# A Perceiver layer on one core: the last two tiles' banks, halves and feature sums, and two layer norms whose scale moves behind the products

## The chip, the core and the metric

The kernel runs on one core of a Trainium2 chip. The metric is the device time of one execution in microseconds, from which a median over runs is taken. Lower is better.

The engines are named as the profile names them: PE is the matrix engine (its weight loads, PEld, overlap with its products), DVE the vector engine, ACT the scalar engine, POOL the general engine, and SP the one whose queue issues most of the DMAs.

## The reference

One latent block x of 128 rows by 512 columns goes through three layers, each of the form x = x + f(layernorm(x)):

```python
# 1: linear cross attention over 12544 context rows, 16 heads of 32, 64 features
q, k, v = heads(layernorm(x) @ Wq.T + bq), heads(ctx @ Wk.T + bk), heads(ctx @ Wv.T + bv)
q_prime, k_prime = relu(q @ Wqf.T), relu(k @ Wkf.T) * mask
kv    = einsum('nf,ne->fe', k_prime, v)      # sum over the 12544 rows, per head
k_sum = sum(k_prime)                         # the same sum of the features alone
x = x + (q_prime @ kv) / (q_prime @ k_sum + 1e-8) @ Wo.T + bo
# 2: gated running average, then a gated feed forward
q, k, v = split(rms(layernorm(x)) @ w_qkv.T); q, k = rms(q), rms(k); w = exp(k)
y = sigmoid(q) * cumsum(w * v) / (cumsum(w) + 1e-6)
u, g = split(y @ w_swiglu.T);  x = x + (u * silu(g)) @ w_out.T
# 3: two experts, the better one weighted by its softmax share, activation max(h, h/2)^2
x = x + share * (max(h, h / 2) ** 2) @ w_proj[e].T     where h = layernorm(x) @ w_fc[e].T
```

## The kernel before

The program is written engine by engine: each engine has its own instruction list, and semaphores order them. Nothing is scheduled automatically, so the order on an engine is the order of the source.

**The long part (0 to about 735 us).** The context comes in 98 tiles of 128 rows, numbered 0 to 97 (NT = 98), four to a period. Per tile PE makes the values (4 steps of 3 products, in `v_bank`, a bank of PSUM), the keys of a tile ahead (in `k_bank`), the features (4 jobs of 2 products in `f_ps`, `feature_job`), and the key-value sums of the tile before (`key_values`, 8 products into `kv_ps`). ACT and DVE empty the banks: for each of the 4 jobs ACT copies a share (`fb`) and DVE adds it (`features_sum`), DVE masks the tile's features (`masked_features`), and ACT and DVE split them into a high and a low part (`features_high`, `features_low`) that `key_values` takes. POOL adds the masked features of each tile onto `ksum_acc`. A feature job i waits until DVE has added job i - 2, since two banks alternate.

**The last two tiles, 96 and 97.** There are no keys left to make, so `values_last` puts one feature job behind each value step. The values of tile 96 go into `k_bank`, those of 97 into `v_bank`. POOL still adds tile 96 onto `ksum_acc`. Then `feature_sums` sums `ksum_acc` and tile 97's features over rows with products against a tile of ones, and the last `key_values` follows.

**The tail (about 754 us to the end).** One chain over 128 rows: denominator and numerator of the attention, the product with Wo (L776), a layer norm, the q, k, v products, two running sums, the feed forward with `hidden_down` (4 calls, all summed in one bank, `down_ps`), a layer norm, the router, and the experts with 8 more calls of `hidden_down`. `turn` transposes a 128x512 block on PE in two halves, `turned` copies them back on DVE. `keep_warm(n)` issues n products whose result nobody reads, while PE would be waiting for the vector chain (L773, L777, L828). These products are full fp32, each of which runs as two instructions. Both layer norms of the tail have DVE take the moments (L1039 to L1042, and L869 to L871), then POOL raise the variance to the power -1/2 (L321), then DVE write (x - mean) * scale in two halves, which `turn` waits for. In the q, k, v part, POOL adds a constant `rms_eps` to the mean squares of k and q (L385).

SP issues the large weight transfers of the tail after the last `key_values`. The names of the semaphores say what they count (`kf_ready`: tiles of masked features; `kv_done`: tiles summed).

## Time and profile before

| | |
|---|---|
| median of 3 runs | 897.54 us (897.27 to 897.81) |
| the profiled execution, its own time | 898.03 us |
| its span, first to last instruction | 896.2 us |
| PE busy in the span | 881.7 us (98%) |
| DVE, ACT, POOL busy | 617.6, 509.3, 369.0 us |
| PE's share of the chain that ended last | 89% |
| granted PE clock, mean | 1.000 |

The execution's own time is its span and about 1.8 us around it. Busy shares are means over a span with two very different stages, the 98 tiles and the tail; the chain of work that ended last says which engine the end waited for at each moment. A granted clock of 1.00 is 2.4 GHz.

### The profile page before, as it was taken

The numbers are of one execution on the slowest core, as the hardware profiler recorded it, in microseconds if no ns is written. First come the engines' busy times: TensorE is split into PE (matmuls) and PEld (weight loads), VectorE is DVE, ScalarE is ACT, GpSimd is POOL, SyncE is SP. The second block draws the span as 40 slices with busy tenths as digits, with TensorE's granted clock in tenths as the row PEclk, the third lists the DMA queues.
The fourth block names the chain that finished last, engine by engine and source line by source line (L and its number), as shares of the span: only waits on it lengthen the run. The fifth ranks groups of instructions, "written<-read, shape, count | busy, mean of one in ns | idle before, by whom it ended". The sixth has DMA issues, their size and how long they took to land.

```text
span 896.2 us, 14101 instructions
## 1 busy us (share of the span) xinstructions
PE 881.7 (98%) x4486; PEld 708.6 (79%) x4486; DVE 617.6 (69%) x992; ACT 509.3 (57%) x916; POOL 369.0 (41%) x212
## 2 busy tenths in 40 slices
PE   8999999999999999999999999999999998999998
PEld 6888888888888888888888888888888887344443
DVE  5777777777777777777777777777777786522422
ACT  5566666666666666666666666666666663100000
POOL 4445555555554444444444444554555341000000
PEclk9999999999999999999999999999999999999999
DMA  6222121212010101010101010101010002936400
GB/s 237 89 77 76 67 81 60 86 55 90 27 47 23 47 23 47 23 47 23 47 23 47 23 47 23 47 23 47 23 48 24 1 28 118 443 146 278 188 1 12
DMA packets 12550, 64.12 MB, mean 72 GB/s; under 512 B 1904, under 2 KB 2672, under 8 KB 11376
## 3 DMA queue, kind: packets, MB, share of 16 engines
q1 hardware_dynamic: 11808, 63.58, 19.1%
q10 hardware_dynamic: 720, 0.25, 0.1%
q8 instruction: 13, 0.21, 0.1%
q14 instruction: 9, 0.07, 0.0%
HBM read 63.56 MB, written 0.26 MB: 71 GB/s over the span
## 4 chain that ended last, share of the span: by engine, by line
PE 89%; issue 6%; DVE 2%; DMA 2%; ACT 1%; SPq 0%; POOL 0%; POOLq 0%; DVEq 0%; ACTq 0%
PE kv_ps L634 10%; PE f_ps L624 10%; PE v_bank L547 10%; PE v_bank L548 10%; PE k_bank L547 10%; PE v_bank L549 10%; PE k_bank L548 10%; PE k_bank L549 9%; PE kv_ps L805 3%; PE v_bank L702 2%; PE k_bank L702 2%; DMA x_sb<-in_x 1%; PE k_bank L688 1%; DVE kf L912 0%; DVE keys L882 0%
## 5 line engine op out<-in xcount | busy, mean ns | idle before, releaser
L335 POOL TENSOR_TENSOR ksum_acc<-ksum_acc,kf 128x1024 f32<-128x1024 f32 x97 | 233.9, 2412 | 193.0 <-DVE kf L906 188.5
L430 ACT ACTIVATE fb<-f_ps 128x256 f32<-128x256 f32 x392 | 149.7, 382 | 177.3 <-PE f_ps L624 171.0
L899 DVE TENSOR_TENSOR kf<-f_ps,fb 128x256 f32<-128x256 f32 x392 | 165.3, 422 | 111.2 <-ACT fb L430 106.0
L328 POOL TENSOR_TENSOR ctx_lo<-ctx_raw,ctx_hi 128x512 fp32r<-128x512 f32 x94 | 123.1, 1310 | 177.7 <-ACT ctx_hi L405 177.7
L624 PEld LDWEIGHTS f_ps<-bd,keys 128*128 128x128 f32 x784 | 146.2, 188 | 35.1 <-DVE kf L899 2.4
L624 PE MATMUL f_ps<-bd,keys 128*128 128x256 f32 x784 | 156.0, 281 | 2.2 <-DVE kf L899 2.2
L547 PE MATMUL v_bank<-wv_hi,ctx_lo 128*128 128x512 f32 x388 | 153.2, 395 | 0.0
L547 PE MATMUL k_bank<-ctx_hi,wk_lo 128*128 128x512 f32 (+1 forms) x392 | 152.8, 390 | 0.0
L548 PE MATMUL v_bank<-wv_lo,ctx_hi 128*128 128x512 f32 x388 | 152.6, 393 | 0.0
L548 PE MATMUL k_bank<-ctx_lo,wk_hi 128*128 128x512 f32 (+1 forms) x392 | 152.2, 388 | 0.0
L549 PE MATMUL v_bank<-wv_hi,ctx_hi 128*128 128x512 f32 x388 | 150.9, 389 | 0.0
L912 DVE TENSOR_TENSOR kf<-kf 128x1024 fp32r<-128x1024 f32 x98 | 122.0, 1245 | 42.0 <-ACT kf L436 42.0
L549 PE MATMUL k_bank<-ctx_hi,wk_hi 128*128 128x512 f32 (+1 forms) x392 | 149.9, 382 | 0.0
L413 ACT ACTIVATE keys<-k_bank,bias_cols 64x512 fp32r<-64x512 f32 (+1 forms) x194 | 131.1, 676 | 30.8 <-PE k_bank L549 28.4
L882 DVE SCALAR_TENSOR_TENSOR keys<-k_bank,bias_cols,keys 64x512 fp32r<-64x512 f32 (+1 forms) x194 | 143.3, 738 | 6.3
L634 PEld LDWEIGHTS kv_ps<-kf,v 128*128 128x128 f32 x784 | 106.3, 189 | 8.4 <-DVE v L890 0.3
L634 PE MATMUL kv_ps<-kf,v 128*128 128x256 f32 x784 | 109.1, 282 | 0.2 <-DVE v L890 0.2
L436 ACT ACTIVATE kf<-kf 128x1024 fp32r<-128x1024 f32 x98 | 103.9, 1061 | 3.6 <-DVE kf L906 1.3
L549 PEld LDWEIGHTS k_bank<-ctx_hi,wk_hi 128*128 128x128 f32 x392 | 73.7, 188 | 15.8
L549 PEld LDWEIGHTS v_bank<-wv_hi,ctx_hi 128*128 128x128 f32 x388 | 72.9, 188 | 16.4
L906 DVE TENSOR_SCALAR kf<-kf,mask 128x1024 f32<-128x1024 f32 x98 | 73.9, 754 | 10.9
L547 PEld LDWEIGHTS k_bank<-ctx_hi,wk_lo 128*128 128x128 f32 x392 | 73.6, 188 | 9.6 <-issue 0.7
(185 smaller groups left out, 792.0 us busy)
## 6 DMA issues: line engine op xcount, KB each, us to landing
ctx_raw<-in_ctx SPq DMA_DIRECT2D x48, 512.0 KB, 3.3
early<-in_early SPq DMA_DIRECT2D x14, 512.0 KB, 4.3
swi_b<-in_swib SPq DMA_DIRECT2D x1, 4096.0 KB, 14.1
w_out<-in_wout SPq DMA_DIRECT2D x1, 4096.0 KB, 23.4
fc<-in_fc SPq DMA_DIRECT2D x1, 4096.0 KB, 34.1
early<-in_proj SPq DMA_DIRECT2D x1, 4096.0 KB, 12.3
swi_b<-in_fc SPq DMA_DIRECT2D x1, 4096.0 KB, 12.3
w_out<-in_proj SPq DMA_DIRECT2D x1, 4096.0 KB, 13.4
```

The costliest lines, as they stand in the source:

```text
L328: pool.tensor_tensor(ctx_lo[:, s, :, cols], ctx_raw[:, :, t % 2 * P:(t % 2 + 1) * P], ctx_hi[:, s, :, cols].bitcast(f32), ALU.subtract).th ...
L335: pool.tensor_tensor(ksum_acc[:, :].rearrange("p (j f) -> p j f", f=P), ksum_acc[:, :].rearrange("p (j f) -> p j f", f=P), kf[:, t % 2, :, ...
L413: act.activation(keys_2[rows, s, 2 * m + h, 0:n], src[rows, 0:n], ACT.Identity, bias=bias_cols[rows, KC + m:KC + m + 1]).then_inc(k_hi_rea ...
L430: act.activation(fb[:, i % 2, :, :], f_ps[i % 2][:, :].rearrange("p (j x f) -> p j x f", j=2, x=2) [:, :, 1, :], ACT.Copy).then_inc(fb_rea ...
L547: pe.matmul(out_ps, st_lo, mv_hi, start=start, stop=False, **kw)
L548: pe.matmul(out_ps, st_hi, mv_lo, start=False, stop=False, **kw)
L549: return pe.matmul(out_ps, st_hi, mv_hi, start=False, stop=stop, **kw)
L624: last = pe.matmul(f_ps[i % 2][:, (j % 2) * 2 * P:(j % 2 + 1) * 2 * P], keys_2[:, s, j, t * P:(t + 1) * P], bd[:, :, :].rearrange("p x f - ...
L634: last = pe.matmul(kv_ps[:, j, :, :].rearrange("p x f -> p (x f)"), v_2[:, t % 2, j, :, :].rearrange("p x e -> p (x e)"), kf_2[:, t % 2, j ...
L882: dve.scalar_tensor_tensor(out=keys_2[other, s, 2 * m + h, 0:n], in0=src[rows, 0:n], scalar=bias_cols[rows, KC + m:KC + m + 1], in1=keys_2 ...
L899: dve.tensor_tensor(kf[:, t % 2, 2 * i:2 * i + 2, :], f_ps[i % 2][:, :].rearrange("p (j x f) -> p j x f", j=2, x=2)[:, :, 0, :], fb[:, i % ...
L912: dve.tensor_tensor(kf_2[:, t % 2, :, 1, :], kf[:, t % 2, :, :], kf_2[:, t % 2, :, 0, :].bitcast(f32), ALU.subtract)\
```

## The change

1. **Banks.** The values of tile 96 go into `v_bank`, those of tile 97 into `k_bank` (before, the other way round), and the feature sums with the denominator's input into `v_bank`.
2. **Order on ACT and DVE in these two tiles.** The values are emptied between feature jobs 2 and 3, where before they came after all four.
3. **Feature sums on PE.** POOL no longer adds tile 96. PE sums `ksum_acc` in two pieces inside tile 97's values, then tile 96's features, then tile 97's: 8 products more.
4. **Tile 97's features in two halves**: mask, high and low part, sums and key-value sums are each done for pairs 0 to 3 and then 4 to 7.
5. **Layer norm scales behind the products.** In both layer norms of the tail DVE writes only x - mean, and `turn` no longer waits for POOL. The scale is multiplied in later: into v's product with the exponentials, into `rms_eps` (now a column that DVE computes), into the router's logits, and its square into the expert shares.
6. **Column halves.** The product with Wo and every `hidden_down` is made as two products of 256 columns in two banks. The adds and moments (`centered`) take each half as it is done. The last call of each sum finishes half 0 before it starts half 1. `keep_warm` goes from 4 to 1 and from 3 to 1. The output's halves are added and stored as they are done.

```diff
@@ banks @@
-        k_ps, v_ps, down_ps = [k_bank[:, :], v_bank[:, :]], [kv_bank[1], kv_bank[2]], kv_bank[0]
+        k_ps, v_ps = [k_bank[:, :], v_bank[:, :]], [kv_bank[1], kv_bank[2]]
+        o_ps = [v_bank[:, 0:D // 2], kv_bank[1][:, 0:D // 2]]
+        half_ps = [kv_bank[0][:, 0:D // 2], kv_bank[3][:, 0:D // 2]]
@@ POOL @@
-            period(LAST, 0, last=True, splits=0)
@@ ACT @@
+            def tile_last(n, t):
+                features_share(n, 0, False)
+                features_high(n - 1, t - 1)
+                for i in (1, 2):
+                    features_share(n, i, False)
+                values_high(n, t, False, k_bank if t else v_bank)
+                features_share(n, 3, False)
@@ PE @@
             def values_last(n, s, t, jobs):
-                if t == 0:
+                pe.wait_ge(v_lo_ready, n - t)
+                if t == 1:
                     pe.wait_ge(k_lo_ready, 2 * KC * (LAST + 1))
-                else:
-                    pe.wait_ge(v_lo_ready, n - 1)
                 for k in range(KC):
-                    value_step(n, s, t, k, k_bank if t == 0 else v_bank)
+                    value_step(n, s, t, k, k_bank if t else v_bank)
                     feature_job(*jobs[k])
+                    if t == 1 and k in (1, 2):
+                        if k == 1:
+                            pe.wait_ge(v_lo_ready, NT - 1)
+                            pe.wait_ge(ksum_added, NT - LAST_TILES)
+                        feature_sums(0, k - 1)
...
-                feature_sums()
-                key_values(NT - 1, LAST_TILES - 1, last_tile=True)
+                for b in range(2):
+                    feature_sums(1, b)
+                for b in range(2):
+                    pe.wait_ge(kf_ready, NT + b)
+                    last = feature_sums(2, b)
+                last.then_inc(ksumT_done, 1)
+                pe.wait_ge(v_lo_ready, NT)
+                for b in range(2):
+                    pe.wait_ge(kf_lo_ready, NT + b)
+                    for j in range(b * NPAIR // 2, (b + 1) * NPAIR // 2):
+                        last = key_value(j, 1, False, True)
+                    last.then_inc(kv_done, 1)
...
-            rows(k_ps[1], act_T, w_o, 0, turned=1).then_inc(o_done, 1)
-            keep_warm(4)
+            for b in range(2):
+                rows(o_ps[b], act_T, w_o, b * D // 2, turned=1, n=D // 2).then_inc(o_done, 1)
+            keep_warm(1)
...
-                for k in range(KC):
-                    last = pe.matmul(down_ps, hid_T2[n % 2][:, k, :], w[:, at + k, :],
+                for b, k in ([(b, k) for b in range(2) for k in range(KC)] if last_one else
+                             [(b, k) for k in range(KC) for b in range(2)]):
+                    last = pe.matmul(half_ps[b], hid_T2[n % 2][:, k, :], w[:, at + k, b * D // 2:(b + 1) * D // 2],
...
-            keep_warm(3)
+            keep_warm(1)
@@ DVE @@
+            def tile_last(n, t):
+                features_sum(n, t, 0, False)
+                features_low(n - 1, t - 1)
+                for i in (1, 2):
+                    features_sum(n, t, i, False)
+                values_low(n, t, k_bank if t else v_bank)
+                features_sum(n, t, 3, False)
+                if t < LAST_TILES - 1:
+                    masked_features(n, t)
...
+            def centered(done, n, ps):
+                for b, cols in enumerate(halves):
+                    dve.wait_ge(done, n + b)
+                    link(dve.tensor_tensor(x1[:, cols], x1[:, cols], ps[b], ALU.add))
+                    link(dve.bn_stats(moments[:, b, :], x1[:, cols]))
+                link(dve.bn_aggr(stat[:, 6:8], moments[:, :, :].rearrange("p b s -> p (b s)")))
+                for cols in halves:
+                    dve.tensor_scalar(att[:, cols], x1[:, cols], stat[:, 6:7], None, ALU.subtract).then_inc(act_ready, 1)
+            centered(o_done, 1, o_ps)
...
+            dve.tensor_scalar(rms_eps[:, :], stat[:, 9:10], RMS_EPS, None, ALU.mult).then_inc(var_ready, 1)
+            turned(2)
             dve.wait_ge(rstd_ready, 2)
...
-            dve.tensor_tensor(wval, v_ps[0], wexp, ALU.mult).then_inc(wval_ready, 1)
+            dve.scalar_tensor_tensor(out=wval, in0=v_ps[0], scalar=stat[:, 9:10], in1=wexp, op0=ALU.mult, op1=ALU.mult)\
...
-            link(dve.tensor_copy(logit[:, 0:2], v_ps[0][:, 0:2]))
+            link(dve.tensor_scalar(logit[:, 0:2], v_ps[0][:, 0:2], stat[:, 8:9], None, ALU.mult))
```

How the instructions stand now. PE at the start of tile 96 (the first two rows are `key_values` of tile 94, the rest values and the first feature job of tile 96), before:

```order
L634 MATMUL kv_ps<-kf,v 128x256 [waits kf_lo_ready,v_lo_ready]
L634 MATMUL kv_ps<-kf,v 128x256 x7
L547 MATMUL k_bank<-wv_hi,ctx_lo 128x512 [waits k_lo_ready]
L548 MATMUL k_bank<-wv_lo,ctx_hi 128x512
L549 MATMUL k_bank<-wv_hi,ctx_hi 128x512
L624 MATMUL f_ps<-bd,keys 128x256 [waits fsum_ready,k_lo_ready]
L624 MATMUL f_ps<-bd,keys 128x256
```

and of the changed kernel:

```order
L648 MATMUL kv_ps<-kf,v 128x256 [waits kf_lo_ready,v_lo_ready]
L648 MATMUL kv_ps<-kf,v 128x256 x7
L553 MATMUL v_bank<-wv_hi,ctx_lo 128x512 [waits v_lo_ready]
L554 MATMUL v_bank<-wv_lo,ctx_hi 128x512
L555 MATMUL v_bank<-wv_hi,ctx_hi 128x512
L635 MATMUL f_ps<-bd,keys 128x256 [waits fsum_ready,k_lo_ready]
L635 MATMUL f_ps<-bd,keys 128x256
```

The bank is another, and the wait is for the values' low part of tile 95 (`v_lo_ready`) where it was for the last keys' low part (`k_lo_ready`).

PE at the end of tile 97: `key_values` of tile 96, feature sums, `key_values` of tile 97, denominator, before:

```order
L634 MATMUL kv_ps<-kf,v 128x256 [waits kf_lo_ready,v_lo_ready]
L634 MATMUL kv_ps<-kf,v 128x256 x7
L649 MATMUL k_bank<-ones,ksum_acc 128x64 [waits ksum_added,v_lo_ready]
L649 MATMUL k_bank<-ones,ksum_acc 128x64 x7
L649 MATMUL k_bank<-ones,kf 128x64 [waits kf_ready]
L649 MATMUL k_bank<-ones,kf 128x64 x7
L634 MATMUL kv_ps<-kf,v 128x256 [waits kf_lo_ready,v_lo_ready]
L634 MATMUL kv_ps<-kf,v 128x256 x7
L744 MATMUL v_bank<-ksum_k,qf_T 128x64 [waits ksum_ready]
L744 MATMUL v_bank<-ksum_k,qf_T 128x64 x7
```

and of the changed kernel, from the same `key_values` on:

```order
L648 MATMUL kv_ps<-kf,v 128x256 [waits kf_lo_ready,v_lo_ready]
L648 MATMUL kv_ps<-kf,v 128x256 x7
L656 MATMUL v_bank<-ones,kf 128x64 x8
L656 MATMUL v_bank<-ones,kf 128x64 [waits kf_ready]
L656 MATMUL v_bank<-ones,kf 128x64 x3
L656 MATMUL v_bank<-ones,kf 128x64 [waits kf_ready]
L656 MATMUL v_bank<-ones,kf 128x64 x3
L648 MATMUL kv_ps<-kf,v 128x256 [waits kf_lo_ready,v_lo_ready]
L648 MATMUL kv_ps<-kf,v 128x256 x3
L648 MATMUL kv_ps<-kf,v 128x256 [waits kf_lo_ready]
L648 MATMUL kv_ps<-kf,v 128x256 x3
L761 MATMUL v_bank<-ksum_k,qf_T 128x64 [waits ksum_ready]
```

Tile 96's features are summed here now (the row without a wait), tile 97's sums and key-value sums are in halves, and the sums of `ksum_acc` have moved up into the values.

DVE around the first layer norm of the tail, from the add of x and bo to the copies of the transposed block, before:

```order
L1032 TENSOR_TENSOR x<-x_sb,bo 128x512
L1034 TENSOR_TENSOR x<-x,v_bank 128x512 [waits o_done,vector_chain]
L1039 BN_STATS stat<-x 128x6 [waits vector_chain]
L1040 BN_AGGR stat<-stat 128x2 [waits vector_chain]
L1041 TENSOR_SCALAR stat<-stat 128x1 [waits vector_chain]
L1042 TENSOR_SCALAR stat<-stat 128x1
L1046 TENSOR_SCALAR att<-x,stat 128x256 [waits rstd_ready]
L1046 TENSOR_SCALAR att<-x,stat 128x256
L1028 COPY act_T<-kv_ps 128x256 [waits actT_done]
L1028 COPY act_T<-f_ps 128x256 [waits actT_done]
```

and of the changed kernel:

```order
L1071 TENSOR_TENSOR x<-x_sb,bo 128x512
L1077 TENSOR_TENSOR x<-x,v_bank 128x256 [waits o_done,vector_chain]
L1078 BN_STATS moments<-x 128x6 [waits vector_chain]
L1077 TENSOR_TENSOR x<-x,kv_ps 128x256 [waits o_done,vector_chain]
L1078 BN_STATS moments<-x 128x6 [waits vector_chain]
L1079 BN_AGGR stat<-moments 128x2 [waits vector_chain]
L1081 TENSOR_SCALAR att<-x,stat 128x256 [waits vector_chain]
L1081 TENSOR_SCALAR att<-x,stat 128x256
L1084 TENSOR_SCALAR stat<-stat 128x1
L1085 TENSOR_SCALAR stat<-stat 128x1
L1086 TENSOR_SCALAR rms_eps<-stat 128x1 [waits vector_chain]
L1067 COPY act_T<-kv_ps 128x256 [waits actT_done]
```

The wait for `rstd_ready` (POOL) ahead of the two writes of `att` is gone, the adds and moments are in halves, and three small operations stand between the second write of `att` and the first copy.

## Rows read from the trace of the kernel before

**Rows 1.** Busy time by window: stretch, its length, PE, PEld, DVE, ACT, POOL, PEclk, DMA, GB/s

```profile
730.00:760.00 30.00, 25.82 (x182) 23.10 (x181) 20.00 (x35) 13.02 (x26) 9.16 (x6) 1.00 0.25 89
...
786.00:829.00 43.00, 42.97 (x112) 19.91 (x113) 8.32 (x13) 3.67 (x5) 0.00 (x0) 1.00 0.52 208
...
835.00:896.00 61.00, 58.12 (x160) 27.00 (x158) 18.32 (x33) 5.08 (x9) 0.00 (x0) 1.00 0.10 39
```

**Rows 2.** Chain of work that ended last, a main-loop tile: start us, us, what

```profile
728.84 0.95 PE kv_ps L634 x8
729.79 0.23 PE v_bank L547
...
730.48 0.24 PE f_ps L624 x2
```

**Rows 3.** Timeline, 734 to 755 us: start, length, engine, operation, count, idle time before it

```profile
734.81 1.12 PE L634 MATMUL kv_ps<-kf,v 128*128 128x256 f32 x8
...
736.31 1.00 DVE L882 SCALAR_TENSOR_TENSOR keys<-k_bank,bias_cols,keys 64x256 fp32r<-64x256 f32 x2
...
737.37 0.50 PE L547 MATMUL k_bank<-wv_hi,ctx_lo 128*128 128x512 f32 x1 [1.44 <-DVE keys L882]
...
738.17 0.40 PE L624 MATMUL f_ps<-bd,keys 128*128 128x256 f32 x2
...
738.61 0.38 ACT L430 ACTIVATE fb<-f_ps 128x256 f32<-128x256 f32 x1 [2.64 <-PE f_ps L624]
...
739.01 1.06 ACT L436 ACTIVATE kf<-kf 128x1024 fp32r<-128x1024 f32 x1
...
739.12 0.42 DVE L899 TENSOR_TENSOR kf<-f_ps,fb 128x256 f32<-128x256 f32 x1 [1.81 <-ACT fb L430]
...
740.11 1.22 DVE L912 TENSOR_TENSOR kf<-kf 128x1024 fp32r<-128x1024 f32 x1 [0.56 <-ACT kf L436]
...
751.00 1.95 PE L649 MATMUL k_bank<-ones,kf 128*128 128x64 f32 x16
...
753.15 1.22 PE L634 MATMUL kv_ps<-kf,v 128*128 128x256 f32 x8 [0.20 <-DVE v L890]
```

**Rows 4.** Waits between 730 and 896 us: who waited for whom, us in total, times, longest

```profile
PE f_ps L624 <- DVE kf L899: 2.0, 2, 1.3
```

**Rows 5.** Timeline of PE and DVE around the first layer norm of the tail

```profile
766.54 3.60 PE L688 MATMUL k_bank<-x_sb,ident 128*128 128x512 f32 x8
...
766.81 0.69 DVE L1034 TENSOR_TENSOR x<-x,v_bank 128x512 f32<-128x512 f32 x1 [3.00 <-PE v_bank L702]
...
767.53 0.69 DVE L1039 BATCH_NORM_STATS2 stat<-x 128x6 f32<-128x512 f32 x1
...
768.26 0.18 DVE L1040 BATCH_NORM_AGGREGATE stat<-stat 128x2 f32<-128x6 f32 x1
...
769.52 0.73 DVE L1046 TENSOR_SCALAR att<-x,stat 128x256 f32<-128x256 f32 x2 [0.83 <-POOL stat L321]
...
769.99 0.44 PE L769 MATMUL kv_ps<-ident,att 128*128 128x128 f32 x2
...
771.03 0.67 PE L702 MATMUL v_bank<-early,act_T 128*128 128x512 f32 x1 [0.28 <-DVE act_T L1028]
```

**Rows 6.** Timeline around the second layer norm of the tail

```profile
829.09 2.74 PE L688 MATMUL k_bank<-x_sb,ident 128*128 128x512 f32 x6
...
829.29 0.69 DVE L1079 TENSOR_TENSOR x<-x,kv_ps 128x512 f32<-128x512 f32 x1 [6.18 <-PE kv_ps L805]
...
832.23 0.44 PE L769 MATMUL kv_ps<-ident,att 128*128 128x128 f32 x2 [0.40 <-DVE att L874]
```

**Rows 7.** Chain of work that ended last, its end: start us, us, what

```profile
886.25 6.88 PE kv_ps L805 x16
```

**Rows 8.** Timeline of DVE at the end of the span

```profile
893.16 0.75 DVE L1107 TENSOR_TENSOR hid<-x,kv_ps 128x256 f32<-128x256 f32 x2 [6.18 <-PE kv_ps L805]
```

**Rows 9.** Groups of PE's instructions by shape: busy us, mean ns, idle time before

```profile
L688 PE MATMUL k_bank<-ksum_acc 128*128 128x512 f32 x12 | 7.5, 787 | 1.9 <-POOL ksum_acc L317 1.9
```

More of the change, by code:

```diff
@@ L337, in add_features, with period @@
                     .then_inc(ksum_added, 1)
[L339 removed]
+            def period(c, s, splits=TILES):
                 n = TILES * c
[L342 removed]
+                for t in range(TILES):
                     if t < splits:
                         split_ctx_low(n + 2 * TILES + t, s, t)
[L345 to L346 removed]
+                    add_features(n + t, t)
             for b in range(2):
@@ L493, in _ @@
             period(LAST - 1, 1, splits=0, keys=HALF)
-            period(LAST, 0, last=True, splits=0)
+            for t in range(LAST_TILES):
+                tile_last(NT - LAST_TILES + t, t)
+            for b in range(2):
+                features_high_last(b)
             act.wait_ge(ksumT_done, 1)
@@ L701, in rows @@
                         pe.wait_ge(actT_ready, 2 * turned - 1 + k // 2)
-                    last = pe.matmul(ps, act_t[:, k, :], w[:, k, at:at + D], start=start and k == 0,
+                    last = pe.matmul(ps, act_t[:, k, :], w[:, k, at:at + n], start=start and k == 0,
                                      stop=stop and k == KC - 1)
@@ L992, in _ @@
             period(LAST - 1, 1, keys=HALF)
-            period(LAST, 0, last=True)
-            dve.wait_ge(kv_done, NT)
+            for t in range(LAST_TILES):
+                tile_last(NT - LAST_TILES + t, t)
+            dve.wait_ge(fsum_ready, JOBS * NT)
+            for b in range(2):
+                masked_features_last(b)
+            for b in range(2):
+                features_low_last(b)
+            dve.wait_ge(kv_done, NT + 1)
             for b in (2, 3):
```

133 lines of the change are left out of this document (58 added, 75 removed).

## The prediction

> **What bounds the kernel now.** I read the page first: PE is busy for 98% of the span. Then I cut the end of the span into windows. From 786 to 829 us PE is busy 42.97 of 43 us, from 835 to 896 us 58.12 of 61, but from 730 to 760 us only 25.82 of 30 [rows 1]. So in the two long product stretches only PE's own pace counts, and what a faster vector chain can win lies where PE waits: around tiles 96 and 97 and around the layer norms. The 96 tiles ahead of 735 us are not touched, and I take them as they are. The chain of work gives PE's pace there: a value step takes 0.69 us (729.79 to 730.48), a feature job 0.24, a `key_values` 0.95 [rows 2]. A timeline row of PE reads longer, since the end of its last product is modelled (1.12 for the same 0.95), so I count from start to start.
>
> The timeline then shows the waits. `key_values` of tile 94 starts at 734.81 and so hands over at 735.76, but tile 96's values start at 737.37, after DVE's last keys (736.31 and 1.00 long) [rows 3]. Two feature jobs wait another 2.0 us for DVE [rows 4], and the last `key_values` starts at 753.15, after 0.20 of wait [rows 3]. In the tail, the products of `keep_warm` only fill the time of the vector chain, which has the same length with or without them [rows 5, 6].
>
> **Part A, tiles 96 and 97.** Before: from 735.76 to 754.10 (753.15 + 0.95) are 18.34 us. The work in it is 8 value steps (5.52), 8 feature jobs (1.92), 3 `key_values` (2.85) and 16 sum products. Eight sum products take about 1.87 (the row says 1.95 with its modelled end [rows 3]), so 3.74, and the work is 14.03. The remaining 4.3 us are waits and slow first products after them.
>
> After, step by step. Values 96 need only `v_bank` free, which is long so: they start at 735.76. The first feature job starts at 736.45. ACT takes its share 0.44 after a job starts (738.17 to 738.61), so 736.89 to 737.27; DVE leaves the keys at 737.31 and adds until 737.8; ACT's high part of tile 95 (1.06) runs until 738.35, DVE's low part (1.22) until 739.6, the second add (0.42, or 0.37 in a queue) until 740.0 [rows 3]. Feature job 3 waits for that add. PE has done its third other job and four value steps at 739.26, so one wait of 0.8 us stays, 1.03 with the slow first product. Behind it I followed every wait in the same way: the next adds are ready 1.1 us or more ahead of the jobs that need them, tile 97's masked first half 0.6 ahead of its sums, and its low parts 1.1 ahead of the last `key_values`. So from 740.04 on PE never waits. The price is one more block of sums, 1.87, all on PE. Sum: 14.03 + 1.87 + 1.03 = 16.93 instead of 18.34, and the last `key_values` starts at 751.74 instead of 753.15: **1.41 us won**. DVE's low part of tile 96 also loses its overlap with POOL's add, but PE does not wait for it. What follows (denominator, transposes, numerator, SP's four weight transfers) moves as one block. ksum's copy on ACT ends at about 752.6, where PE is free at 752.7, so it hides, by 0.1 only. Bounds: 0.6 if one more feature wait of 0.8 us comes in, 1.8 if the remaining wait falls to half.
>
> **Part B, the first layer norm.** Before, from DVE's add at 766.81 to the transposes at 769.99 are 3.18 us: add 0.69, moments 0.69, aggregate 0.18, two small ones, POOL's power, then 0.47 from `att`'s start to the transpose [rows 5]. After, half 0's add and moments run while PE makes half 1. Behind half 1 stand an add of 128x256 (0.42, as the row of that shape [rows 3]), moments of 256 columns, the aggregate 0.18 and three gaps of 0.03. No row has moments of half size: 0.35 (half of 0.69) to 0.69, and I take 0.42, as for the add. That is 1.11, and 1.58 with the 0.47. Gain 1.60. `keep_warm(1)` ends after 0.86 (829.09 and 829.29 show that it starts 0.2 ahead of the add [rows 6]) and is no longer what PE waits in. Against it: three small operations (0.37 together with their wait) stand ahead of the first copy and end 0.2 later than the transpose allows. Part B wins **1.40**. The column halves also make two instructions of 256 columns out of each of 512; that price comes below.
>
> **Part C, the second layer norm.** From the add at 829.29 to the transpose at 832.23 are 2.94 us [rows 6], afterwards again 1.58: gain **1.36**. Here only one small operation stands in between and fits into the 0.47. The router's logits need POOL's power, which ends about 0.5 after the transpose starts, with the copies and the router products still to come: hidden. The shares are needed only after the first expert product, 3.4 us away.
>
> **Part D, the end.** DVE adds the output's two halves back to back, 0.75 for both where one takes 0.42 [rows 8]. Half 0 is now done during half 1's products, so **0.33** is won.
>
> **Part E, the halved products.** 16 instructions of 512 columns take 6.88 us, 0.430 each [rows 7]. At the granted 2.4 GHz and two cycles per column in full fp32 (1024 cycles, 0.4267) that is an excess of 0.003 per instruction. For 256 columns the sum is bounded by two rows. Below, the same 0.003: 16 x 0.2163 - 3.44 = 0.02 per call. Above, the excess of the only 256-column products in the trace, those of `key_values`: 0.119 against 256 cycles or 0.1067, 0.012 [rows 2], so 16 x 0.2253 - 3.44 = 0.17. There are 13 such products (4, 8 and Wo). That makes 0.3 to 2.2; I take 0.4, near the lower, because the row nearest in kind is full fp32. The new form of v's product on DVE I put at 0.03.
>
> The Trainium skill, TensorE: Matmul & The Clock Gate, Part 1 ("Wait — 56ns, not 53.3ns?"), gives a fixed 2.5 ns per matmul, an estimate of 0.3 us for Part E; the trace's 3 ns agree, and its 12 ns row does not. The skill's VectorE: DVE Perf Modes (the errata-adjusted table) speaks against halves, since latency between instructions is paid per tile: two halves at 0.42 are 0.84 against 0.69 in one, and the trace agrees. Here one of the two lies under PE's products, so only the second counts.
>
> **Sum.** 1.41 + 1.40 + 1.36 + 0.33 = 4.50 won, 0.43 paid, net 4.07. The profiled execution's 898.03 would be 893.96; it lies 0.49 above the median, so for a median I predict **893.5 us**. A measurement of this kernel tells about 0.2% (1.8 us) from no change.
>
> **The rivals.**
> - *Halved products at the pace of the 256-column rows*: PE-bound stretches [rows 1] take every ns. Then E costs 2.2: 895.3. Against: the nearer row. 6 in 100.
> - *A new wait in Part A*, such as ksum's copy or a feature job coming late, takes most of its gain: 894.6 to 894.9. For: the chain ACT, DVE, PE there has slack of only 0.1 to 0.6 at two places. 6 in 100.
> - *The clock falls.* At the launch, behind idle time, PE's first 12 instructions of 512 columns take 7.5 us [rows 9] where 12 x 0.430 are 5.2: 2.3 us lost. `keep_warm` shrinks by 3 and 2 products, which opens idle gaps of about 1.1 and 0.8 us around each layer norm's transposes. One fall gives 895.8, two 898.1: no change. Against: PE waited 1.44 us at 737 with the clock at 1.00 [rows 1, 3], and the numerator's part leaves gaps too. The same page of the Trainium skill, Part 1, has the clock follow PE's activity and fall when idle; that rule would make this rival true, and the launch rows agree with it, while the short gaps here do not show it. 7 in 100.
> - *Slower: the weight load shows.* Each 256-column product needs its own weight load, and its time to hide in is halved. The gain is gone at an excess of 4.1 / 208 = 20 ns more per instruction, a pace of 0.236. If the load shows by the 0.117 us at which sum products follow each other (1.87 / 16), the 208 instructions cost 24 us: 918; by a third of that, about 901.6. Against: those sums show loads of full fp32 every 0.117 us, below 0.213. 5 in 100.
> - *My forecast*, 76 in 100, with a range of its own of 892.6 to 894.9.
>
> **How the numbers follow.** Forecast, first and second rival are faster by over 1.8 us: 0.88. The clock rival is no change: 0.07. The last is slower: 0.05. The range takes the forecast's own and reaches to the second and first rival and the edge of one fall of the clock: 892.3 to 895.8.
>
> **What would show it.** Right: values 96 start within 0.1 of `key_values` 94's end; one feature wait below 1 us; `key_values` 97 about 1.4 earlier; add of half 1 to the transpose in about 1.6 twice; calls of `hidden_down` at 3.45 to 3.5. Wrong: calls at 3.6 or more; a granted clock under 1.00 behind a layer norm; a second wait of `f_ps` or of the sums; q, k, v's running sum waiting longer on ACT or POOL, which share the place of the scale now.

## The result, and the profile after

The changed kernel takes **893.25 us** (median of 6 runs, 893.02 to 894.96) where the kernel before takes 897.79 beside it (6 runs, 897.27 to 899.45): a ratio of 0.9953, 95% interval 0.994 to 0.9966. That is 4.5 us won, more than twice what this measurement can tell from nothing. The prediction was 893.5 us. The profiled execution of the changed kernel took 893.13 us, with a span of 891.3 and a mean granted clock of 1.000, against 898.03 and 896.2 before: 4.9 us less span.

The first view is the busy time by window of the changed kernel (stretch, its length, PE, PEld, DVE, ACT, POOL, granted PE clock, DMA share, GB/s, as in [rows 1]):

```profile
730.00:760.00 30.00, 28.50 (x202) 25.55 (x202) 20.63 (x39) 13.22 (x27) 6.72 (x5) 1.00 0.29 108
786.00:829.00 43.00, 41.59 (x144) 24.99 (x143) 11.36 (x22) 3.67 (x5) 0.54 (x1) 1.00 0.54 214
835.00:891.00 56.00, 53.75 (x213) 37.13 (x211) 16.57 (x26) 4.18 (x7) 0.00 (x0) 1.00 0.05 22
```

In the first window PE is busy 28.50 of 30 us where it was 25.82. The second window holds less PE time because the second layer norm now starts 3 us earlier (826.13 for 829.29), so that its waits fall into this window.

The timeline of the changed kernel, tiles 96 and 97, answers to [rows 3]:

```profile
734.52 1.12 PE L648 MATMUL kv_ps<-kf,v 128*128 128x256 f32 x8
735.48 0.40 PE L553 MATMUL v_bank<-wv_hi,ctx_lo 128*128 128x512 f32 x1
...
736.07 2.39 POOL L336 TENSOR_TENSOR ksum_acc<-ksum_acc,kf 128x1024 f32<-128x1024 f32 x1 [3.72 <-DVE kf L923]
...
738.11 1.44 DVE L929 TENSOR_TENSOR kf<-kf 128x1024 fp32r<-128x1024 f32 x1 [0.56 <-ACT kf L434]
...
740.03 0.48 PE L635 MATMUL f_ps<-bd,keys 128*128 128x256 f32 x2 [0.92 <-DVE kf L916]
...
743.80 1.22 DVE L929 TENSOR_TENSOR kf<-kf 128x1024 fp32r<-128x1024 f32 x1 [0.42 <-ACT kf L434]
...
747.78 3.68 PE L656 MATMUL v_bank<-ones,kf 128*128 128x64 f32 x32
...
751.27 1.20 PE L648 MATMUL kv_ps<-kf,v 128*128 128x256 f32 x8
751.50 0.77 ACT L508 ACTIVATE ksum_k<-v_bank 64x256 f32<-64x256 f32 x2 [1.36 <-PE v_bank L656]
...
752.32 2.00 PE L761 MATMUL v_bank<-ksum_k,qf_T 128*128 128x64 f32 x16
```

`key_values` of tile 94 starts at 734.52 and the values of tile 96 0.96 later, with no wait in their row. One feature job waits 0.92 for DVE. After it PE has no row with a wait up to and including the last `key_values` (751.27). From `key_values` of 94 to that of 97 are 16.75 us; before they were 18.34.

The first layer norm of the tail, to be laid beside [rows 5]:

```profile
765.05 0.42 DVE L1077 TENSOR_TENSOR x<-x,kv_ps 128x256 f32<-128x256 f32 x1 [0.84 <-PE kv_ps L719]
765.51 0.43 DVE L1078 BATCH_NORM_STATS2 moments<-x 128x6 f32<-128x256 f32 x1
765.97 0.21 DVE L1079 BATCH_NORM_AGGREGATE stat<-moments 128x2 f32<-128x12 f32 x1
766.21 0.61 DVE L1081 TENSOR_SCALAR att<-x,stat 128x256 f32<-128x256 f32 x2
766.62 0.44 PE L786 MATMUL kv_ps<-ident,att 128*128 128x128 f32 x2 [0.82 <-DVE att L1081]
766.75 0.14 DVE L1084 TENSOR_SCALAR stat<-stat 128x1 f32<-128x1 f32 x1
...
766.99 0.15 DVE L1086 TENSOR_SCALAR rms_eps<-stat 128x1 f32<-128x1 f32 x1
767.10 0.43 DVE L1067 COPY act_T<-kv_ps 128x256 f32<-128x256 f32 x1
...
767.67 1.10 PE L719 MATMUL v_bank<-early,act_T 128*128 128x512 f32 x2 [0.35 <-DVE act_T L1067]
```

From the add to the transpose are 1.57 us where there were 3.18. The second layer norm, beside [rows 6], shows the same 1.57 (826.13 to 827.70) where there were 2.94:

```profile
826.13 0.42 DVE L1077 TENSOR_TENSOR x<-x,kv_ps 128x256 f32<-128x256 f32 x1 [0.91 <-PE kv_ps L824]
...
827.70 0.44 PE L786 MATMUL kv_ps<-ident,att 128*128 128x128 f32 x2 [0.82 <-DVE att L1081]
...
828.98 1.05 PE L851 MATMUL kv_ps<-w_router,act_T 128*128 128x2 f32 x8 [0.59 <-DVE act_T L1067]
829.90 3.68 PE L719 MATMUL k_bank<-fc,act_T 128*128 128x512 f32 x8
```

The chain of work that ended last, one call of `hidden_down` and the last two (beside [rows 7]; start us, us, what):

```profile
855.97 3.46 PE kv_ps L824 x16
...
881.84 6.92 PE kv_ps L824 x32
```

DVE's timeline, its last row (beside [rows 8]):

```profile
888.79 0.42 DVE L1147 TENSOR_TENSOR hid<-x,kv_ps 128x256 f32<-128x256 f32 x1 [1.31 <-PE kv_ps L824]
```

The last row of the chain is two calls of `hidden_down`: 16 products of 256 columns (32 instructions) take 6.92 us, so an instruction takes 6.92 / 32 or 0.2163. DVE has one half of the output left to add behind them where it had two. The table lays the span's 4.9 us against the terms of the prediction, each as a difference of starts in the two timelines.

| part | predicted | measured |
|---|---|---|
| ahead of tile 96: `key_values` 94 at 734.52 for 734.81 | 0 | 0.29 |
| A: tiles 96 and 97, 18.34 to 16.75 | 1.41 | 1.59 |
| A: the denominator's products, 1.73 to 1.84 (ksum's copy) | 0 | -0.11 |
| B: add to transpose, and transpose to q, k, v's product | 1.40 | 1.60 |
| C: add to transpose, second layer norm | 1.36 | 1.37 |
| D: end of PE's last product to the end of the span, 3.07 to 2.54 | 0.33 | 0.53 |
| E: halved products and v's product | -0.43 | -0.39 |
| sum | 4.07 | 4.88 |

The first row is no effect of the change: nothing ahead of tile 96 was touched. There the transfer of the block x takes 10.20 us instead of 10.46 (by the chain of work, issued at 3.18 and 3.15 us), and what follows is earlier by about as much. In the profiled executions of the experiments the start of this `key_values` lies between 733.86 and 734.72, so a difference of some tenths of a us between two single executions can come from there.

### The profile page after: what moved, and what is told of

It reads as the page before. It is cut to its first block, busy times and chain, and to the rows that moved or that the text cites. A ratio compares the mean times of both kernels' runs of the same rounds, so it can differ in the third digit from the quotient of the medians.

```text
span 891.3 us, 14331 instructions
## 1 busy us (share of the span) xinstructions
PE 878.6 (99%) x4596; PEld 728.0 (82%) x4596; DVE 618.5 (69%) x1000; ACT 509.4 (57%) x917; POOL 366.0 (41%) x210
## 4 chain that ended last, share of the span: by engine, by line
PE 95%; DVE 2%; DMA 2%; issue 1%; SPq 0%; ACT 0%; POOL 0%; DVEq 0%; ACTq 0%; POOLq 0%
PE kv_ps L648 10%; PE f_ps L635 10%; PE v_bank L553 10%; PE v_bank L554 10%; PE k_bank L553 10%; PE k_bank L554 10%; PE v_bank L555 10%; PE k_bank L555 10%; PE kv_ps L824 5%; PE v_bank L719 3%; PE k_bank L719 2%; PE kv_ps L719 2%; DMA x_sb<-in_x 1%; PE f_ps L710 1%; PE v_bank L656 1%
## 5 line engine op out<-in xcount | busy, mean ns | idle before, releaser
L336 POOL TENSOR_TENSOR ksum_acc<-ksum_acc,kf 128x1024 f32<-128x1024 f32 x96 | 230.9, 2405 | 188.6 <-DVE kf L923 188.6
L929 DVE TENSOR_TENSOR kf<-kf 128x1024 fp32r<-128x1024 f32 x97 | 120.2, 1239 | 40.6 <-ACT kf L434 40.6
```

The source lines that it names most:

```text
L336: pool.tensor_tensor(ksum_acc[:, :].rearrange("p (j f) -> p j f", f=P), ksum_acc[:, :].rearrange("p (j f) -> p j f", f=P), kf[:, t % 2, :, ...
L929: dve.tensor_tensor(kf_2[:, t % 2, :, 1, :], kf[:, t % 2, :, :], kf_2[:, t % 2, :, 0, :].bitcast(f32), ALU.subtract)\
```

## The experiments

Eleven kernels were run. Each is the changed kernel with the edit shown, unless it says otherwise; the code is shortened, and `...` marks what is left out. "Full clock" means executions with a mean granted clock of 1.000; why this matters is said behind the third experiment. The kernel before ran beside each group of experiments, and its full-clock median was 897.72 beside the first four, 897.84 beside the next four and 897.83 beside the last three. So between groups a difference of 0.1 us says nothing.

**1. Only the last two tiles changed** (items 1 to 4; layer norms and halves undone, `keep_warm` back at 4 and 3).

```diff
-            for b in range(2):
-                rows(o_ps[b], act_T, w_o, b * D // 2, turned=1, n=D // 2).then_inc(o_done, 1)
-            keep_warm(1)
+            rows(v_bank[:, :], act_T, w_o, 0, turned=1).then_inc(o_done, 1)
+            keep_warm(4)
...
```

> Items 1 to 4 alone (banks, order, sums on PE, tile 97's halves); the tail's products, layer norms and keep_warm are as before. My theory (each stage pays for itself): key_values 97 starts about 16.75 us after key_values 94, where before it was 18.34, and nothing behind it changes, so 1.5 us less than the kernel before. Rival (the tiles' gain comes only together with the tail's new products, since the chain behind absorbs it): within 0.3 us of the kernel before.

Measured: 896.32 us (10 runs), ratio 0.998 (0.9971 to 0.999), against 897.96; three of the ten had a mean clock of 0.998. At full clock it is 896.26 against 897.72, 1.5 us less. Tile 94's to tile 97's `key_values`: 734.57 to 751.32, 16.75 us, the same as with all items. So Part A is worth 1.5 us on its own and does not depend on the tail.

**2. Only the banks swapped** (item 1, on the kernel before).

```diff
...
-                    value_step(n, s, t, k, k_bank if t == 0 else v_bank)
+                    value_step(n, s, t, k, k_bank if t else v_bank)
...
-                        last = pe.matmul(k_bank[:, j * PAIR:(j + 1) * PAIR],
+                        last = pe.matmul(v_bank[:, j * PAIR:(j + 1) * PAIR],
...
```

> Item 1 alone on the kernel before: the two tiles' values and the feature sums change banks, POOL still adds tile 96, the order on ACT and DVE, full tiles and the tail are as before. Theory A (the bank is the whole gain of the tiles): values 96 start with key_values 94's end; feature job 3 of tile 96 waits 0.8 us, job 3 of tile 97 waits 1.3 us because DVE's low part runs beside POOL's add (2.0 us); key_values 97 starts 16.8 us after key_values 94 and the time is 1.4 to 1.5 us less than before. Theory B (the sums on PE and the halves matter): without them the old waits come back behind the first one, key_values 97 starts 17.7 us or more after key_values 94, and the gain is 0.6 us or less.

Measured: 896.24 us (9 runs, none with a fallen clock), ratio 0.9974 (0.9964 to 0.9984). The bank swap alone is nearly all of Part A. Its timeline shows what still waits:

```profile
734.35 1.11 PE L633 MATMUL kv_ps<-kf,v 128*128 128x256 f32 x8
...
739.88 0.48 PE L623 MATMUL f_ps<-bd,keys 128*128 128x256 f32 x2 [0.95 <-DVE kf L898]
...
742.15 2.40 POOL L335 TENSOR_TENSOR ksum_acc<-ksum_acc,kf 128x1024 f32<-128x1024 f32 x1 [2.91 <-issue]
743.63 2.01 DVE L911 TENSOR_TENSOR kf<-kf 128x1024 fp32r<-128x1024 f32 x1 [0.42 <-ACT kf L436]
746.03 0.50 PE L623 MATMUL f_ps<-bd,keys 128*128 128x256 f32 x2 [1.26 <-DVE kf L898]
```

From `key_values` to `key_values` are 16.86 us (734.35 to 751.21). DVE's low part of tile 96 starts while POOL's add runs and takes 2.01 us, and a feature job waits 1.26 behind it. In the changed kernel, without that add, the low part takes 1.22 and the wait is gone, but PE makes 8 products (16 instructions) more.

**3. POOL adds tile 96 again** (item 3 undone).

```diff
@@ POOL @@
+            add_features(NT - LAST_TILES, 0)
@@ PE @@
...
-                        feature_sums(0, k - 1)
...
-                for b in range(2):
-                    feature_sums(1, b)
+                    feature_sums(0, b)
```

> The changed kernel with item 3 undone: POOL adds tile 96 again, PE sums ksum_acc once, behind key_values 96 (8 sum products fewer on PE). Theory A (the sums on PE cost what they save): 1.76 us of PE's work goes, DVE's low part of tile 96 is at 1.7 to 2.0 us instead of 1.22, feature job 3 of tile 97 waits 1.2 us, key_values 97 starts 16.3 us after key_values 94 where the changed kernel has 16.75: 0.4 us less than the changed kernel. Theory B (moving the sums to PE is what wins): key_values 97 starts 17.2 us or more after key_values 94, 0.5 us or more over the changed kernel.

Measured: 734.65 to 751.02, 16.37 us, 0.38 less than the changed kernel. This repeats in two later kernels with the same item undone (16.40 and 16.39). So the feature sums on PE cost more than they save: 16 instructions, which take 1.76 us, remove a wait of 1.2 and a slow first product behind it. The times alone did not show this. Four executions took 892.69, 894.36, 894.59 and 894.59 us, ratio 0.9947 (0.993 to 0.9964), and only the first had a granted clock of 1.000. The profiled one was among the others. Its windows (stretch, length, PE, PEld, DVE, ACT, POOL, PEclk, DMA, GB/s) and PE's timeline:

```profile
829.00:831.00 2.00, 2.00 (x11) 1.25 (x11) 0.73 (x5) 0.30 (x1) 0.00 (x0) 0.82 0.62 262
831.00:833.00 2.00, 2.00 (x4) 0.94 (x3) 0.96 (x6) 0.00 (x0) 0.00 (x0) 0.50 1.21 524
833.00:835.00 2.00, 2.00 (x5) 0.80 (x4) 0.00 (x0) 0.00 (x0) 0.00 (x0) 0.83 1.18 508
```

```profile
827.47 0.44 PE L783 MATMUL kv_ps<-ident,att 128*128 128x128 f32 x2 [0.82 <-DVE att L1078]
...
828.75 1.05 PE L848 MATMUL kv_ps<-w_router,act_T 128*128 128x2 f32 x8 [0.59 <-DVE act_T L1064]
829.66 5.38 PE L716 MATMUL k_bank<-fc,act_T 128*128 128x512 f32 x8
```

The granted clock falls to 0.50 (1.2 GHz) behind the second layer norm and the router, and the first expert product takes 5.38 us instead of 3.68: 1.7 us lost. Ahead of that, PE has had a wait of 0.8 us, transposes, a wait of 0.6 and eight small products. This is the clock rival of the prediction, in some executions and not in others. Of the changed kernel's own six executions two have a mean clock of 0.998 and take 894.87 and 894.96, the other four 893.02 to 893.36. Before the change it happens too: of the 52 executions of the kernel before that ran beside the experiments, 18 have a mean clock of 0.998 or less and take some 1.6 us more.

**4. No column halves** (item 6 undone, `keep_warm(2)` twice, since the chain is longer).

```diff
-                for b, cols in enumerate(halves):
-                    dve.wait_ge(done, n + b)
-                    link(dve.tensor_tensor(x1[:, cols], x1[:, cols], ps[b], ALU.add))
-                    link(dve.bn_stats(moments[:, b, :], x1[:, cols]))
+                dve.wait_ge(done, n)
+                link(dve.tensor_tensor(x1[:, :], x1[:, :], ps, ALU.add))
+                link(dve.bn_stats(moments[:, 0, :], x1[:, :]))
...
```

> The changed kernel with item 6 undone: the products with Wo and hidden_down in 512 columns and one bank, adds and moments over the whole row, both keep_warm at 2. The scales stay behind the products. My theory: from DVE's add to the transposes 2.12 us instead of 1.57 at both layer norms, the end 0.5 us later, calls of hidden_down back at 3.43 (0.3 us in all): 1.3 us over the changed kernel, 3.2 us under the kernel before. Rival (halving pays nothing, since its second instruction per column pair costs what the earlier start gives): within 0.3 us of the changed kernel.

Measured: 894.45 us (5 runs), ratio 0.9964 (0.9949 to 0.9978); at full clock 894.29, 1.2 more than the changed kernel's 893.09. From the add to the transpose there are 2.08 us (826.32 to 828.40) instead of 1.57, and a call of `hidden_down` takes 3.43 to 3.44 instead of 3.46. So the halves win 0.5 in each layer norm and 0.3 to 0.5 at the end, and cost 0.2 to 0.3 of pace. The expectation of 1.3 us was met.

**5. Scales back in front of the products** (item 5 undone, `keep_warm(2)` twice).

```diff
...
+                last.then_inc(var_ready, 1)
+                dve.wait_ge(rstd_ready, 2 if done is o_done else 3)
+                at = 9 if done is o_done else 8
                 for cols in halves:
-                    dve.tensor_scalar(att[:, cols], x1[:, cols], stat[:, 6:7], None, ALU.subtract).then_inc(act_ready, 1)
+                    dve.tensor_scalar(att[:, cols], x1[:, cols], stat[:, 6:7], stat[:, at:at + 1], ALU.subtract, ALU.mult)\
...
```

> The changed kernel with item 5 undone: DVE waits for POOL's power and writes (x - mean) * scale in both layer norms; the halves stay; both keep_warm at 2. My theory: from the add of half 1 to the transposes about 2.5 us instead of 1.57 at both layer norms, less the 0.2 us by which the first copy was late: 1.6 us over the changed kernel, 2.9 under the kernel before. Rival (POOL's power overlaps with something else now, or the filler products bound it): under 0.5 us over the changed kernel.

Measured: 895.17 us (9 runs), ratio 0.997 (0.9959 to 0.998), 2.1 more than the changed kernel at full clock. Add to transpose: 2.68 and 2.43 us instead of 1.57 twice, so 1.97 in sum. The expectation of 1.6 took 2.5 twice, 1.86 in sum, and then took off 0.2 for a first copy that is late in the changed kernel. That was the miss: the copy is not late there (0.48 behind the transpose, and 0.47 here). The other 0.1 are the writes of `att`: two with subtraction and multiplication take 0.73, with subtraction alone 0.61.

```profile
828.46 0.15 DVE L1083 TENSOR_SCALAR stat<-stat 128x1 f32<-128x1 f32 x1
828.69 0.54 POOL L324 TENSOR_TENSOR stat<-stat,half 128x1 f32<-128x1 f32 x1 [50.14 <-DVE stat L1083]
829.27 0.73 DVE L1090 TENSOR_SCALAR att<-x,stat 128x256 f32<-128x256 f32 x2 [0.65 <-POOL stat L324]
```

**6 and 7. `keep_warm` at 4 and 3 as before (shown), and at 0 and 0.**

```diff
-            keep_warm(1)
+            keep_warm(4)
...
-            keep_warm(1)
+            keep_warm(3)
```

> The changed kernel with keep_warm back at 4 and 3. Theory A (the filler products are now longer than the chain they fill): 3.43 and 2.57 us of them stand behind products whose transposes are wanted 1.84 us later, so the transposes start 1.6 and 0.7 us later: 2.3 us over the changed kernel. Theory B (the clock needs them): no loss, or a gain, and a granted clock of the changed kernel that was under 1.00 in the gaps.

> The changed kernel with no keep_warm behind the product with Wo and behind the feed forward. Theory A (no fall): PE stands idle 1.8 us at both places, the products behind it still follow at 0.430 us, time within 0.2 us of the changed kernel. Theory B (the clock falls when PE idles): products behind one or both gaps follow at up to 0.86 us, 2.3 us or more over the changed kernel.

Measured: with 4 and 3, 895.52 us (7 runs, 895.22 to 895.88), ratio 0.9972 (0.9961 to 0.9984). The filler now lasts longer than the vector chain, and PE's transposes start 3.16 and 2.30 us behind the add of half 1 instead of 1.57 (765.16 to 768.32 and 827.78 to 830.08). That is 2.3 us, as Theory A said, and the time is 2.4 more than the changed kernel's at full clock. At the second layer norm the transposes now have no wait:

```profile
830.08 0.38 PE L786 MATMUL kv_ps<-ident,att 128*128 128x128 f32 x2
```

Without filler, 895.0 us (8 runs, 893.2 to 896.72), ratio 0.9965 (0.9952 to 0.9978): 893.2 at full clock, but six executions lie at 894.6 to 895.0 (clock 0.998) or 896.3 to 896.7 (0.996). One of the latter was profiled:

```profile
827.00:829.00 2.00, 0.73 (x5) 0.43 (x5) 1.64 (x6) 0.00 (x0) 0.54 (x1) 0.92 1.05 311
829.00:835.00 6.00, 6.00 (x13) 3.53 (x14) 1.68 (x10) 0.30 (x1) 0.00 (x0) 0.50 1.00 431
835.00:838.00 3.00, 3.00 (x8) 1.41 (x7) 0.51 (x1) 0.60 (x1) 0.00 (x0) 0.92 0.76 328
```

Here the clock falls at about 828.7 us, by the first window's 0.92, while PE waits between the transposes and the router's products. That is earlier than in experiment 3 (about 830.3, in the first expert product), and it stays low for longer. At the first layer norm of this execution PE waits as long (1.68 us at both), and the clock stays at 1.00 there. Of the two theories neither holds as it stands: the time is Theory A's in two executions, Theory B's in three, and between the two in three. So filler there has a use after all: more than fits under the chain delays PE, and none lets the clock fall in most executions.

**8. Quarters**: each product of `hidden_down` of 256 columns in two of 128.

```diff
-                    last = pe.matmul(half_ps[b], hid_T2[n % 2][:, k, :], w[:, at + k, b * D // 2:(b + 1) * D // 2],
...
+                    for c in range(2):
+                        last = pe.matmul(half_ps[b][:, c * P:(c + 1) * P], hid_T2[n % 2][:, k, :],
+                                         w[:, at + k, b * D // 2 + c * P:b * D // 2 + (c + 1) * P],
...
```

> The changed kernel with every hidden_down made of four products of 128 columns per k, two in each of the two banks (32 instructions more than the changed kernel's 16 would be at full width: 32 a call). Theory A (a fixed 0.003 us per instruction): 32 x 0.110 = 3.52 a call instead of 3.46, 12 calls, 0.7 us over the changed kernel. Theory B (a weight load bounds an instruction at 0.117 us): 3.74 a call, 3.4 us over. Theory C (the load is not hidden at all): calls of 5 us or more, over 18 us over.

Measured: 895.4 us (8 runs, 894.48 to 896.32), ratio 0.9972 (0.9961 to 0.9982); at full clock 894.62, 1.5 more than with halves, and four executions with a fallen clock (one execution of over 3000 us, unexplained, is left out). From the chain of work:

```profile
819.34 7.16 PE kv_ps L825 x64
```

64 instructions of 128 columns take 7.16 us, 0.1119 each, against 0.1067 at two cycles per column of the full clock: an excess of 0.005 where 256 columns have 0.003 and 512 columns 0.003. The 12 calls cost 0.11 to 0.12 each, 1.4 in all, where Theory A had 0.7. A load bound of 0.117 (Theory B) and a load that is not hidden (Theory C) are excluded. But whether the excess beyond 0.003 is the product's or the weight load's stays open: the feature sums, with only 64 columns each, follow each other at 0.110 (3.52 / 32), which is close to 0.1119.

**9 to 11. Filler that fits.** The ninth has `keep_warm(2)` at both layer norms and one filler product of 256 columns between the transposes and the router. The tenth has the same and POOL adds tile 96 (as in 3). The eleventh is the tenth without the 256-column product, and the router's products stand behind the first expert product.

```diff
-            keep_warm(1)
+            keep_warm(2)
...
+            pe.matmul(k_bank[:, 0:D // 2], ident[:, :], x_sb[:, 0:D // 2], start=True, stop=True)
             pe.wait_ge(actT_ready, 8)
             for k in range(KC):
                 last = pe.matmul(v_ps[0][:, 0:2], act_T[:, k, :], w_router[:, k, :], start=k == 0,
...
```

> The changed kernel with one more filler product at each layer norm (2 calls of keep_warm instead of 1) and one filler product of 256 columns between the last transposes and the router's products. Theory A (the clock falls in some executions because TensorE has too little to do between the second layer norm and the router, and filler there prevents it): no execution with a granted clock under 1.000, and a time within 0.4 us of the full-clock executions of the changed kernel (893.1), as the filler fits into TensorE's waits. Rival B: the falls have nothing to do with this stretch; then about 1 execution in 3 stays at 0.998 and 1.8 us longer. Rival C: the second filler call does not fit, and moves transposes and all behind by up to 0.3 us at each layer norm: 893.7.

> The version with tile 96's features added whole by GpSimd (its full-clock execution took 892.69) and the same filler as in the kernel sent beside it. Theory A: 892.7 in all executions, 0.4 less than the kernel beside it, clock 1.000 throughout. Rival B: the gain of 0.4 at tiles 96 and 97 is chance; then both are equal. Rival C: falls of the clock stay, 1 in 3.

> As the kernel beside it, but the router's eight products stand behind the first expert product, so that no low stretch of eight small products follows the transposes, and no filler is put there. Theory A: TensorE no longer waits about 0.6 us for the last copy of the transposes with nothing to do in it, as the expert product begins on the copies that are there: 0.3 us less than the kernel beside it, 892.4, if the chain of the gates' logits stays under the second expert product. Rival B: the exponential's table load (1.28 us) and the exponential come after ScalarE's first half scale and hold up the first expert's features; then 0.25 to 0.9 us more than the kernel beside it, 893.0 to 893.6. The clock: no falls if their cause is the low stretch; 1 in 3 otherwise.

Measured, each with 5 runs against 897.96 before:

| kernel | median | range | ratio | clock under 1.000 |
|---|---|---|---|---|
| 9, filler fitted | 893.06 | 893.02 to 893.34 | 0.9941 (0.9927 to 0.9955) | 0 of 5 |
| 10, and POOL adds tile 96 | 892.82 | 892.20 to 893.03 | 0.9939 (0.9925 to 0.9952) | 0 of 5 |
| 11, router later | 892.85 | 892.65 to 893.04 | 0.9938 (0.9924 to 0.9951) | 0 of 5 |

PE's timeline of the tenth around the second layer norm:

```profile
825.71 1.02 PE L702 MATMUL k_bank<-x_sb,ident 128*128 128x512 f32 x2
...
826.70 0.44 PE L783 MATMUL kv_ps<-ident,att 128*128 128x128 f32 x2
...
827.24 0.60 PE L846 MATMUL k_bank<-x_sb,ident 128*128 128x256 f32 x2
...
827.98 1.05 PE L849 MATMUL kv_ps<-w_router,act_T 128*128 128x2 f32 x8
828.90 3.68 PE L716 MATMUL k_bank<-fc,act_T 128*128 128x512 f32 x8
```

The transposes and the router's products no longer have a wait in their rows, and the first expert product starts 2.20 us behind the first transpose, as it did with the wait (827.70 to 829.90). The filler costs nothing: the ninth takes 893.06, as the changed kernel does at full clock (893.09). The falls, by kernel, beside the wait that PE's transposes at the second layer norm have in the profiled execution:

| kernel | wait ahead of the transposes, us | executions with a fallen clock |
|---|---|---|
| before; experiment 1; experiment 2 | 0.40 to 0.41 | 18 of 52; 3 of 10; 0 of 9 |
| changed; experiments 3 and 8 | 0.81 to 0.82 | 2 of 6; 3 of 4; 4 of 8 |
| experiments 4 and 5, `keep_warm(2)` | 0.40; 0.83 | 2 of 5; 3 of 9 |
| experiment 7, no filler | 1.68 | 6 of 8 |
| experiments 6, 9, 10, 11 | none | 0 of 7; 0 of 5; 0 of 5; 0 of 5 |

Where PE has no wait there, none of 22 executions fell; with one, 41 of 111 did. That is a count over kernels that differ in other ways too, not an experiment on this wait alone. The calls of `keep_warm` alone do not sort the kernels, since 4 and 3 calls stand on both sides. Neither does the wait ahead of the router's products, which experiment 6 has too (0.63). It stays open whether a single kernel's count says much: experiment 2 has the wait and none of its 9 executions fell. And only two fallen executions were profiled, so that for the others the place of the fall is not shown.

The tenth is the fastest, but only 0.24 below the ninth, where the stretch of tiles 96 and 97 is 0.36 shorter (16.40 against 16.76). The ranges overlap, so it is the stretch in the traces that shows the difference, and the time does not contradict it. Its lowest time, 892.20, is that of the profiled execution, in which tile 94's `key_values` starts at 733.86, 0.8 us ahead of the ninth's; that is not of the edit.

The eleventh gains and loses. Its first expert product starts 1.05 us behind the first transpose. But then the gates come late:

```profile
832.91 1.28 ACT L548 ACT_TABLE_LOAD   x1
...
834.21 0.30 ACT L548 ACTIVATE logit<-logit 128x2 f32<-128x2 f32 x1
...
835.89 0.75 DVE L1143 SCALAR_TENSOR_TENSOR hid<-gate,logit 128x512 f32<-128x512 f32 x1
...
836.70 0.66 PE L707 MATMUL f_ps<-ident,hid 128*128 128x128 f32 x4
```

The exponential's table load and the chain behind it make `hid` start 8.35 us behind the first transpose (827.54) where in the tenth it is 7.34 (834.04 behind 826.70), and PE's next transposes follow the start of the second expert product by 3.79 us instead of 3.44. The router's products have only moved: they now take 0.88 us behind the first expert product. So 1.15 us are won ahead of it and 0.88 and 0.35 lost behind it, and from the first transpose to the third expert product both kernels need about the same, 9.66 and 9.58. The hold-up that Rival B named is what happened, but smaller than the 0.25 us it said at the least; Theory A's gain of 0.3 did not come.

## Why the prediction was right, and where it was off

The time and the mechanisms were right. The medians differ by 4.5 us where 4.07 was predicted, and what was off are sizes. That 893.25 lies only 0.25 below 893.5 is partly luck: every part came out a little better than predicted, but beside the changed kernel the one before took 897.79, not the 897.54 from which the prediction started, and two executions with a fallen clock lift the median over the full-clock 893.09.

- **Part A: 1.59 for 1.41, less 0.11.** Three things were mis-sized. The one wait is 0.92, not 0.8: DVE's low part of tile 95 takes 1.44, since it now starts 0.35 before POOL's add ends (738.46), and the 1.22 of [rows 3] was measured behind that add. Against that, 16 sum instructions take 1.76 (3.52 for 32 in the chain of work), not 1.87, which is 0.33 for three blocks. That ksum's copy hides, "by 0.1 only", failed, though by little: the copy ends at 752.27, and only at 752.32 does the denominator start, its first weight load together with its first product. Before, that load started 0.12 ahead (754.09 for a product at 754.21). The block of 16 instructions takes 1.84 instead of 1.73. What the prediction did not see is how the gain divides. Experiment 2 shows the bank swap alone at 1.5, and experiments 2 and 3 together that the order and the halves win 0.49 more (16.86 to 16.37) and that the sums on PE give 0.38 back.
- **Part B: 1.60 for 1.40.** The term that failed is the late copy. The prediction took three small operations of 0.37 and put the copy 0.2 late. The two writes of `att` without a multiplication take 0.61 instead of 0.73, so DVE is free sooner. The last of the three small operations starts at 766.99 and the copy at 767.10, 0.48 behind the transpose, as it did before (0.47).
- **Part C: 1.37 for 1.36.** The half-size moments take 0.43 (0.42 taken), the aggregate of two sets 0.21.
- **Part D: 0.53 for 0.33.** Besides DVE's 0.33, the second half's transfer is done 0.2 sooner behind its add (2.09 instead of 2.29 us from the add's end to the end of the span). Why is not tested.
- **Part E: 0.39 paid for 0.43.** The pace is 0.2163, the lower bound. The 12 ns of excess of the key-value rows belongs to that other kind of product. Experiment 4 agrees from the other side. The fixed 2.5 ns of the Trainium skill, TensorE: Matmul & The Clock Gate, Part 1, stands beside measured 3 ns at 512 and 256 columns and 5 ns at 128.
- **The rivals.** No new wait in Part A, no 256-column pace, no weight load: shown by rows. The clock rival, given 7 in 100, was true in part. Two of the changed kernel's 6 executions have a fallen clock and take 1.8 us more, where 2.3 was predicted for one fall; that it falls behind the second layer norm is shown in the profiled executions of experiments 3 and 7, not in its own. What the prediction missed is that it is a matter of single executions, and that the kernel before has such executions too (18 of 52). So it moves both medians little, and the difference stays. The argument against it was that PE had waited 1.44 us at 737 without a fall. That wait stands between full products, the one at the second layer norm ahead of transposes and a further wait. That this makes the difference is a reading, not shown: in experiment 7 the first layer norm has transposes behind the same wait of 1.68 us, and no fall.
- **Not of the change:** 0.29 us of the two profiled spans' difference arise ahead of tile 96, 0.26 of them in a transfer at the launch. The sum without them is 4.59; the medians at full clock, 897.82 (31 executions) and 893.09 (4), differ by 4.7.

Open stays where the clock falls in the kernel before, whose profiled execution had the full clock, and why one execution falls and the next of the same program does not.

## What to carry to other kernels

Look at which buffer the first instruction of a stage needs and what was last written to it: one swap of two banks was worth 1.5 us here, a third of the whole change, while the larger rework around it gained 0.1 net. A scale per row can go behind a linear product whenever the vector chain ahead of the product is what TensorE waits for, and a last product can be cut by columns at 1% of its time if the chain behind it is thereby halved. Filler products should be as long as the wait they stand in. When a chain is shortened, measure several executions with their granted clock: too much filler cost 2.1 to 2.8 us in every execution here, too little 1.4 us or more in some.

## What was not expected of the hardware

- The granted clock falls to 1.2 GHz in some executions only, of the same program, behind waits of 0.8 and 0.6 us around the transposes (windows of experiment 3) or behind a wait of 1.7 and inside the one that follows it (experiment 7). One fall costs 1.4 to 1.9 us, or 3.1 to 3.5 when it stays low for longer. In the 22 executions of the four kernels without a wait ahead of those transposes it did not happen, in the others in 41 of 111.
- Full fp32 products cost 0.430, 0.2163 and 0.1119 us per instruction at 512, 256 and 128 columns, so at two cycles per column the excess is 3 to 5 ns. At 64 columns they cost 0.110 us, hardly less than at 128.
- DVE's low part of 128x1024 takes 1.22 us alone. Where it starts while POOL's add of 128x1024 still runs, it ends 1.08 to 1.09 us after that add ends, however early it started: it takes 1.44 when it starts 0.35 before the add's end (738.11 and 738.46 in the changed kernel) and 2.01 when it starts 0.92 before (743.63 and 744.55 in experiment 2). The same 1.08 to 1.09 stands in all eight kernels whose rows were compared. It reads as if most of DVE's work waited for the end of POOL's; why is not shown.
- A write of 256 columns with subtraction alone takes about 0.06 us less than with subtraction and multiplication (0.61 against 0.73 for two).
